# A mixture-of-experts kernel: one weight load, two small stores and the row gathers change their places

## The reference, cut to what matters

```python
y = einsum('bsi,io->bso', x * ys[:, None, :], weight) * d[:, None, :]
router_probs = softmax(y @ router_w.T + router_b + 0.1 * expert_weights)
top_p, top_i = top_k(router_probs, 2); top_p = top_p / top_p.sum(-1)
h = gelu(einsum('bsd,edh->bseh', y, w1) + b1)
expert_out = einsum('bseh,ehd->bsed', h, w2) + b2
out = x + (top_p[..., None] * take_along_axis(expert_out, top_i)).sum(2)
```

## Time and profile before

| what | us |
| --- | --- |
| time, median of 3 runs (302.75 to 306.69) | 303.74 |
| the profiled execution: its own time | 302.91 |
| its span, first to last instruction | 301.2 |
| TensorE busy in the span | 277.1 (92%) |
| VectorE / ScalarE / GpSimd busy | 202.7 / 196.0 / 169.1 |
| DMA: moved, mean rate | 35.72 MB, 119 GB/s |

### The profile page before, as it was taken

How to read it: one execution, slowest core, us unless ns; L and a number is a source line. 1 busy time by engine, 2 the same in 40 slices (tenths; PEclk the granted TensorE clock), 3 DMA queues, 4 the chain that set the end, 5 groups by cost and what they waited for, 6 DMA issues and landing times.

```text
span 301.2 us, 9047 instructions
## 1 busy us (share of the span) xinstructions
PE 277.1 (92%) x3103; PEld 230.9 (77%) x3103; DVE 202.7 (67%) x459; ACT 196.0 (65%) x425; POOL 169.1 (56%) x159
## 2 busy tenths in 40 slices
PE   7899967999999999999999999999999999999800
PEld 5778967688899998888888888888888878887500
DVE  3956785799999997665665765765756665756510
ACT  3446369499897997576566666666665766675500
POOL 8100036800878668767667667667677567655330
PEclk9799977899999999999999999999999999999985
DMA  6799995599764224232322322422422322412220
GB/s 163 305 400 381 359 291 163 179 351 413 264 181 73 38 39 69 41 71 38 56 56 38 58 54 38 62 50 38 68 40 41 70 39 39 72 21 23 32 33 1
DMA packets 24104, 35.72 MB, mean 119 GB/s; under 512 B 4144, under 2 KB 19968, under 8 KB 23904
## 3 DMA queue, kind: packets, MB, share of 16 engines
q1 hardware_dynamic: 16544, 24.75, 23.7%
q0 software_dynamic: 7488, 10.39, 21.0%
q10 hardware_dynamic: 32, 0.01, 0.0%
HBM read 27.61 MB, written 9.64 MB: 124 GB/s over the span
## 4 chain that ended last, share of the span: by engine, by line
PE 84%; DMA 7%; POOL 1%; DVE 1%; issue 1%; SPq 1%; ACT 0%; DVEq 0%; POOLq 0%
PE ps L611 35%; PE ps L628 29%; PE ps L511 5%; PE ps L529 4%; PE ps L620 4%; PE ps L603 3%; DMA out<-onehot,idx 3%; DMA wsp<-in_L_ffn_w 3%; DMA wsp<-in_x 2%; PE ps L593 1%; SPq L340 1%; PE ps L484 1%; PE ps L493 1%; DVE wsp L862 1%; POOL out L442 1%
## 5 line engine op out<-in xcount | busy, mean ns | idle before, releaser
L611 PE MATMUL ps<-onehot,wsp 128*128 128x128 f16 x1872 | 157.1, 219 | 0.1
L788 ACT ACTIVATE pay<-ps,cur 128x128 f32<-128x128 f32 x312 | 117.2, 462 | 59.2 <-issue 42.2
L611 PEld LDWEIGHTS ps<-onehot,wsp 128*128 (+1 forms) x1872 | 131.6, 96 | 31.4 <-issue 0.3
L628 PE MATMUL ps<-wsp,pay 128*128 (+1 forms) x616 | 138.5, 314 | 1.2 <-DVE pay L1072 1.2
L442 POOL DMA_INDIRECT out<-onehot,idx x39 | 73.0, 1871 | 19.6 <-POOL onehot L433 10.4
L1072 DVE SCALAR_TENSOR_TENSOR pay<-pay,cur 128x512 f16<-128x512 f32 x72 | 54.9, 763 | 28.5 <-ACT pay L776 27.2
L433 POOL TENSOR_SCALAR onehot<-onehot,cur 128x256 f32<-128x256 f32 x37 | 37.9, 1025 | 55.2 <-DVE onehot L1090 37.0
L416 POOL DMA_INDIRECT rows<-y_rows,idx x39 | 44.4, 1137 | 13.4 <-issue 11.6
L628 PEld LDWEIGHTS ps<-wsp,pay 128*128 128x128 f16 x616 | 48.4, 96 | 3.6 <-issue 1.6
L1066 DVE TENSOR_SCALAR pay<-pay,cur 128x512 f16<-128x512 f32 x36 | 20.3, 565 | 27.6 <-ACT pay L788 27.6
L776 ACT ACTIVATE pay<-pay,cur 128x512 f16<-128x512 f32 x36 | 26.0, 722 | 1.2
(11 more groups left out here) (176 smaller groups left out, 215.1 us busy)
## 6 DMA issues: line engine op xcount, KB each, us to landing
stage<-in_L_ffn_w SPq DMA_DIRECT2D x9, 1024.0 KB, 10.3
wsp<-in_L_ffn_w SPq DMA_DIRECT2D x7, 1024.0 KB, 11.6
y_rows<-pay SPq DMA_DIRECT2D x4, 512.0 KB, 9.5
wsp<-in_x SPq DMA_DIRECT2D x3, 512.0 KB, 8.3
b2bc<-in_L_ffn_b SPq DMA_DIRECT2D x1, 1024.0 KB, 7.7
rows<-y_rows,idx POOLq DMA_INDIRECT x39, 3.0
out<-onehot,idx POOLq DMA_INDIRECT x39, 4.0
wsp<-in_x SPq DMA_DIRECT2D x2, 256.0 KB, 5.6
```

Of the source, the lines that this page charges most:

```text
L611: last = mm(ps[:, HB + (2 * j + g) % RING, c * P:(c + 1) * P], wsp[:, bass.ds(e, 1), o:o + P].rearrange("p a f -> p (a f)"), xsp[:, j % RI ...
L628: last = mm(ps[:, OB + j % 2, 0:width], hsp[:, (2 * j + g) % NH, part, c, :], wsp[:, bass.ds(e, 1), o + w:o + w + width].rearrange("p a f ...
L788: last = a.activation(to, ps[:, HB + (2 * j + g) % RING, c * P:(c + 1) * P], ACT.Gelu, bias=cur[:, j % CURS, cc:cc + 1], scale=cur[:, j % ...
```

## The change

Three edits. SP loads half 7 directly behind half 3. The two p stores are issued by GpSimd, right behind the instruction that makes p. In GpSimd's program the gathers of tiles 5 and 6 both stand ahead of the loop, and the loop issues the gather of tile j + 7 in place of tile j + 5; what a gather waits for is the same as before for the same tile (the tile five before it).

```diff
+AHEAD = 2
@@ block.sync
             load_weights(3)
-            sp.wait_ge(p_ready, 1)
-            for b in range(NB):
-                sp.dma_start(y_tiles[:, b, :, D:ROW], payv[:, b * TB:(b + 1) * TB, D:ROW]).then_inc(p_written, 16)
             load_weights(7)
@@ block.gpsimd
             g.tensor_tensor(pex, pex, over(pe1[:, 1, :], E), ALU.mult).then_inc(p_ready, 1)
+            pool.wait_ge(p_ready, 1)
+            for b in range(NB):
+                g.dma_start(y_tiles[:, b, :, D:ROW], payv[:, b * TB:(b + 1) * TB, D:ROW]).then_inc(p_written, 16)
             scale_early(1)
             scale_early(2)
@@
+            def gather_next(j):
+                pool.wait_ge(t_done, j - ROWS + 1)
+                pool.wait_ge(cur_ready, j - ROWS + 1)
+                gather(j)
+
             for j in range(ROWS):
                 gather(j)
+            for j in range(ROWS, ROWS + AHEAD):
+                gather_next(j)
             for j in range(NT):
-                if j + ROWS < NT:
-                    pool.wait_ge(t_done, j + 1)
-                    pool.wait_ge(cur_ready, j + 1)
-                    gather(j + ROWS)
+                if j + ROWS + AHEAD < NT:
+                    gather_next(j + ROWS + AHEAD)
```

## The result

| what | before | after |
| --- | --- | --- |
| median of 22 runs each (range), us | 304.52 (302.47 to 308.29) | 302.19 (301.41 to 305.28) |
| profiled execution: time, span, us | 302.91, 301.2 | 301.68, 300.0 |
| TensorE's mean granted clock | 0.961 | 0.973 |

The ratio of the changed kernel to the one before is 0.9946 (95% interval 0.9919 to 0.9972): some 1.6 us faster, and within 2%. The ratio compares means, with the one slow execution (308.29) left out; the medians are 2.3 us apart. The forecast was 302.0 and a gain of 1.4 us; both came out closely.

What follows compares the result with a forecast made beforehand. TensorE's own matmuls bound the kernel from 57 us on, so only an earlier first tile pays. 302.91 - 1.4 (edit 1) + 0 + 0 = 301.5, 302.3 by the median; predicted 302.0 us, range 300.7 to 307.5.

Steps and rivals of the forecast that it cites:

- The path up to 57 us: Chain ahead of tile 0's first matmul (56.97): p, SP's two p stores, half 7, its matmuls, warming matmuls, transposes.
- edit 1's gap: TensorE's idle 1.00 us before half 7's matmuls in `gram(3)`; loading half 7 behind half 3 was to remove it.
- The clock: Without the gap TensorE's clock may rise sooner, shortening the warming matmuls from 2.56 to 1.28 us; gain 1.0 to 1.8.
- the list of signs: What would show the forecast right (tile 0 at 55.2 to 56.0) or wrong (TensorE waiting for a gather in 54 to 65).
- What is late next: nothing in `gram(3)`: Behind half 7 no other load was to be late in `gram(3)`, which ran 48.59 to about 52.0; gain 1.00 us.
- Edit 2's price: GpSimd's time to issue the two p stores at 41.15: 2 us each, 4 in all, hidden, so cost 0.
- The cover: GpSimd's idle time before the first gather, 3.17 + 1.85 = 5.0 us, within which the p stores cost nothing.
- The dear stores: Rival, slower: p stores beyond 5.0 us on GpSimd delay the gathers; at 5.5 us each, 308.5 us; chance 0.22.
- Edit 3 at nothing: Gathers issued two tiles higher up: nobody waited for one before, so no gain, and cost 0.
- the gathers mattered: Rival, faster: a row waits on a gather unseen in the profile; every tile gains a little, 299 or less; chance 0.04.
- The sum: Profiled execution 302.91 - 1.4 + 0 + 0 = 301.5; by the median 302.3; predicted 302.0.
- The gain taken back: Rival, no change: p's pieces or tiles 2 and 3's gathers come late, TensorE waits 1 to 1.8 us elsewhere; chance 0.12.

## Why the prediction was right, and which step was not

- **The path up to 57 us, and edit 1's gap.** Right: the wait of 1.00 us is gone. The landing was put at 47 to 49 us and is 49.7; in time, by less than I thought. One premise was wrong: half 3's data was to be over by 45.4, when the first p store landed, but half 3 landed at 46.3 (36.43 + 9.9), after that store. The reason given, that half 7 sits behind the stores' small pieces, fits, but no run isolates it, and "the load can be issued when half 3's issue is over ... 5.7 us sooner" is not what pays: with the p stores on GpSimd 2.25 us sooner is enough to close the gap (0.9958), and 4.6 us with p still on SP lose the gain (1.0034). The queue was the right one; the gain was put down to edit 1 where it needs edit 2.
- **The clock.** Right in kind. I took 1.4 us, half way between clock as before (1.0) and clock sooner (1.8). It rose sooner, and the start of tile 0 moved by 2.05, more than the 1.8, because tile 1's rows landed in 2.71 us where 3.0 had been taken. So tile 0 started at 54.9, before the 55.2 to 56.0 named as the sign; and TensorE waited 0.74 us for tile 1's gather at 54.48, which the list of signs had as one of being wrong, though the sum itself had the gathers set this start.
- **"What is late next: nothing in `gram(3)`".** True of `gram(3)`, and too short a look. "SP then reaches its wait for the gathers of tiles 0 to 2 earlier, which ends when they land, so half 12 and what follows do not move by this" is right about what ends SP's wait, but half 12 did move (57.59 in place of 55.99). The same part had the gather of tile 2 fall under L910, landing at 57.6, at "cost 0, at the worst 0.5": half 12 waits for that landing, and half 10 behind it cost 0.88. The same wait for the gather of tile 2 makes half 12 late in the late course of the kernel before. I priced the late gather by TensorE's need of it alone, and forgot the second one that waits for it, SP.
- **Edit 2's price.** Right side, mis-sized: 2 us for each store, 1.04 measured, 2.08 in place of 4 for both. The cover was 5.0; the scalings (44.14, 48.24), ScalarE's split of half 6 (49.50) and the first gather (50.34) stand where they stood. The dear stores did not happen (1.04 each, where 3.4 was the point of no gain). p landed in 5.5 to 6.3 us, a little slower than SP's, and nobody waited for it.
- **Edit 3 at nothing.** The step that failed: "Nobody waited for one before, so nothing is gained". The row is true of one execution. In the late course of the same kernel TensorE waits 1.57 us, and the edit alone measures 0.9965 (1.1 us). "The cover is TensorE's backlog" overlooked the first indirect store ahead of tile 6's gather, which waits for the copy of x. The rival "the gathers mattered" had this mechanism half (a gather's wait that the profile does not say), with 0.04 and a gain in every tile; it is one tile, and not in every execution. Its cost is zero as forecast: in 100 to 280 us TensorE is busy 179.96 us, 179.92 before.
- **The sum.** -1.4 was forecast for the profiled execution, and -1.2 is measured (2.05 less 0.88). The runs' 1.6 us are a mean over two courses with different causes, which the forecast did not know. Two errors, nothing for the gathers and nothing for half 10, had opposite signs; that the total came so near was luck in part.
- **The gain taken back** (0.12): half right. A wait of 0.88 us did appear elsewhere, from the gather of tile 2 under L910 as the rival had it, but through SP's queue and not at TensorE's door, and it took back less than half.

## What to carry to other kernels

Look at what stands ahead of a late load in its queue. Here 2048 pieces of 32 bytes stood ahead of 1 MB, and another order in the same queue was no cure: behind the load the small stores were late themselves (TensorE waited 4.30 us). Another queue was. After a wait is taken away, go through everyone who waits for each step that moves, the queues too, and not only the engine that sets the end. And profile the kernel before more than once, and read which course an execution took before comparing two: a wait that one execution lacks can be worth as much as the one it shows.

## What was not expected of the hardware

- A direct DMA on GpSimd of 1024 pieces of 32 bytes takes 1.04 us of its time, hardly more than a gather of 128 rows (0.95), and 256 pieces take 0.75: the fixed part is the larger. On SyncE the same two stores took 1.3 to 2.35 us behind half 3 and 5.75 behind halves 3 and 7.
- Such a store is not held by VectorE as a gather is. In the kernel with eight stores, three start under L1013 with its two inputs in SBUF (47.87 to 50.28) and take 0.76 to 0.78 us, those ahead of it 0.74 to 0.77 (the first 0.96), while gathers that start under L910 or L916 take 1.95 to 3.15 us in place of 0.95, in all runs. The Trainium skill ("SBUF — State Buffer", section "Who interferes with whom") says that such a VectorE instruction contends with GpSimd where GpSimd reads SBUF; the direct stores, with no index to read, and the gathers agree with it. The same page's warning, that VectorE can starve the descriptors of a DMA on GpSimd's queue, did not come true for these stores under these instructions; no run has them under others.
- Transfers of one queue did not land in the order of their issue: in the kernel before, the first p store, issued behind half 3 on SP, landed at 45.4 and half 3 at 46.3.
- Two courses of one program, 2.2 us apart by 27 us, decided in the first 18 us. Three of six late profiles give the granted clock as 0.50 from 8 to 18 us; the other three give 1.00 beside matmuls that are nearly as slow (eight of y's take 3.1 to 3.3 us there, 3.8 at 0.50, 2.04 in the early course).
